# Layer 2's attention: ACT copies the third turn of each cycle ahead of k, q and v, and the third cycle's PSUM banks shift by one place

## The reference, cut to what matters

```
q = (query @ Wq.T + bq).reshape(B, Sq, 16, 16)      # query = layernorm(x)
k = (key @ Wk.T + bk).reshape(B, Skv, 16, 16)       # key = value = ctx_1024
v = (value @ Wv.T + bv).reshape(B, Skv, 16, 16)
q = q * cq + _rotate_half(q) * sq_                  # rotary embedding
k = k * ck + _rotate_half(k) * sk_
scores = jnp.einsum('bqhd,bkhd->bhqk', q, k) * scale
probs = jax.nn.softmax(scores, axis=-1)
ctx = jnp.einsum('bhqk,bkhd->bqhd', probs, v).reshape(B, Sq, H * Dh)
return ctx @ Wo.T + bo
x = x + jnp.tanh(g_xattn[2]) * (the above)
```

## Time and profile before

| what | value |
|---|---|
| median of three runs | 2769.6 us |
| the profiled execution | 2766.18 us, its span 2764.4 us |
| PE busy | 2617.9 us, 95% of the span |
| PEld busy | 1981.6 us, 72% |
| DVE busy | 1547.1 us, 56% |
| ACT busy | 1296.0 us, 47% |
| POOL busy | 642.0 us, 23% |
| layer 2's attention | from about 1320 to 1664 us of the span |

### The profile page before, as it was taken

One profiled execution on the slowest core, in us unless ns is written; L12 is line 12 of the kernel. 1 busy time (PEld: TensorE's weight loads), 2 busy tenths in 40 slices (PEclk: granted clock), 3 DMA queues, 4 the chain that ended last, 5 costly groups with the idle time before them and its releaser, 6 DMA issues. The chain is left out here.

```text
span 2764.4 us, 56714 instructions
## 1 busy us (share of the span) xinstructions
PE 2617.9 (95%) x19818; PEld 1981.6 (72%) x19818; DVE 1547.1 (56%) x4177; ACT 1296.0 (47%) x3610; POOL 642.0 (23%) x626
## 2 busy tenths in 40 slices
PE   6999978999999999989899998999998999989998
PEld 4777756666666666656677766999995777768887
DVE  4777856555555555535787874333235887742222
ACT  4777743343434334331567663333335777732222
POOL 0666661000000000000444431222221111013232
PEclk9999989999999999999999999999999999999999
DMA  3000002000000000010000006999991000059897
GB/s 119 17 23 18 12 2 109 13 13 8 13 7 13 7 13 7 1 34 1 20 18 19 23 7 244 324 334 327 323 326 46 24 18 24 7 201 312 303 312 224
DMA packets 91811, 267.57 MB, mean 97 GB/s; under 512 B 25068, under 2 KB 50804, under 8 KB 77268
## 3 DMA queue, kind: packets, MB, share of 16 engines
q1 hardware_dynamic: 74356, 242.53, 25.4%
q0 software_dynamic: 13632, 18.62, 3.2%
q10 hardware_dynamic: 3616, 3.67, 0.4%
HBM read 248.13 MB, written 16.65 MB: 96 GB/s over the span
## 5 line engine op out<-in xcount | busy, mean ns | idle before, releaser
L825 PEld LDWEIGHTS a_full_ps<-ident,a_probs 112*125 112x125 f32 x2688 | 369.9, 190 | 122.6 <-issue 59.8
L1926 PEld LDWEIGHTS m_banks<-m_x_inT,m_w 128*128 128x128 f32 x3824 | 435.1, 192 | 15.2 <-issue 13.5
L1926 PE MATMUL m_banks<-m_x_inT,m_w 128*128 128x128 f32 x3824 | 442.2, 276 | 1.4 <-ACT m_x_inT L1997 0.9
L936 ACT ACTIVATE a_probs<-a_masked,a_negmax 112x375 f32<-112x375 f32 x512 | 305.4, 598 | 287.7 <-DVE a_negmax L1151 287.7
L825 PE MATMUL a_full_ps<-ident,a_probs 112*125 112x112 f32 x2688 | 417.5, 281 | 16.7 <-ACT a_pT L943 5.6
L1177 DVE COPY a_pT<-a_full_ps 125x448 f32<-125x448 f32 x448 | 277.4, 621 | 233.9 <-PE a_full_ps L825 231.9
L725 PE MATMUL a_full_ps<-attention_room 128*125 128x256 f32 (+1 forms) x960 | 330.0, 472 | 9.6 <-ACT a_qT L926 3.7
L717 PE MATMUL a_full_ps<-attention_room 128*128 128x375 f32 x896 | 325.0, 491 | 13.8 <-PEq L1769 8.6
L1151 DVE CUSTOM_DVE_ANT_0 a_masked<-a_sc_ps,a_mask_add 112x375 f32<-112x375 f32 x512 | 249.7, 544 | 33.2 <-PE a_sc_ps L812 32.0
L936 ACT ACTIVATE a_probs<-a_sc_ps,a_negmax 112x375 f32<-112x375 f32 x384 | 216.6, 575 | 89.4 <-DVE a_negmax L1157 89.3
L843 PEld LDWEIGHTS a_o_ps<-a_pT,a_v 125*32 125x32 f32 (+1 forms) x5376 | 165.2, 118 | 127.0 <-issue 98.7
(11 more groups left out here) (253 smaller groups left out, 3473.3 us busy)
## 6 DMA issues: line engine op xcount, KB each, us to landing
m_w<-in_L2f_w SPq DMA_DIRECT2D x105, 1024.0 KB, 6.4
m_w<-in_L3f_w SPq DMA_DIRECT2D x72, 768.0 KB, 5.9
attention_room<-in_ctxT SPq DMA_DIRECT2D x64, 375.0 KB, 3.1
m_w<-in_L3f_w SPq DMA_DIRECT2D x36, 640.0 KB
m_b<-in_L2f_b SPq DMA_DIRECT2D x35, 128.0 KB, 8.0
p_rows<-normed SPq DMA_DIRECT2D x16, 224.0 KB, 6.2
attention_room<-in_L0x_spline_wT SPq DMA_DIRECT2D x1, 2048.0 KB, 10.5
net_room<-in_L1f_w SPq DMA_DIRECT2D x2, 1024.0 KB
```

The source lines that it names most:

```text
L825: mm = pe.transpose(full_ps[0:KT, bank_of["turn", i, k], (j % 4) * S:(j % 4 + 1) * S], probs[:, i % 2, a, t * KT:(t + 1) * KT], ident[0:S, ...
L936: act.activation(probs[:, i % 2, a, 0:SK], src, ACT.Exp, bias=negmax[:, m:m + 1], scale=-1.0 if mask else 1.0, accum_out=rowsum[:, par, n: ...
L1926: mm = pe.matmul(ab_ps[:, (par * FC + f) % RING, i * SLOTS:(i + 1) * SLOTS], w[:, par, c, f * P:(f + 1) * P], x_inT[:, c, :], start=(c == ...
```

## The change

ACT's body for layer 2 copied, in the first two cycles, k or q first and the third turn last; in the third cycle k 1 stood between the two pairs of exponentials. Now, in all four cycles, the third turn is copied directly behind the last exponential; in the first three cycles k, q and v follow it, and k 1 no longer stands between the exponentials. In the fourth cycle v 1 stays between the pairs, and v 2 follows the turn. In the table of the ring, the rest of the third cycle moves from the head of that cycle to the end of its second turn's place.

```
--- before
+++ after
@@ CYCLES, layer 2
     2: [[[], [("k", 0)], [], [("rest",), ("xT",)]],
         [[], [("q", 0)], [("out",), ("rest",)], []],
-        [[("rest",)], [("k", 1)], [("v", 0, 0)], []],
+        [[], [("k", 1)], [("v", 0, 0), ("rest",)], []],
         [[], [("v", 1, 0)], [("v", 2, 0)], [("rt",)]]],
@@ act body
                         for group in groups:
                             exps(*group, (0, 1))
                         if exists(t) and not copies_last:
                             copy_turn(t, i)
-                        if divided and (not copies_last or i >= 2):
+                        if divided and (not copies_last or i == NG - 1):
                             copies(t, par, i, 1)
                         for group in groups:
                             exps(*group, (2, 3))
                         if copies_last:
-                            if i < 2:
+                            if exists(t):
+                                copy_turn(t, i)
+                            if i < NG - 1:
                                 copies(t, par, i, 1)
                             copies(t, par, i, 2)
-                            if exists(t):
-                                copy_turn(t, i)
```

## The result

The changed kernel takes 2799.03 us, the median of four runs (2798.84 to 2799.22), against 2769.8 of before. The ratio is 1.0105, 95% interval 1.0093 to 1.0118: slower by 29.2 us, where the prediction said 34.6 (2804 us, in the range 2786 to 2814). The profiled execution took 2799.1 us around a span of 2797.3.

What follows compares the result with a forecast made beforehand. PE was taken as the bound. 0.68 + 0.61 + 1.15 = 2.44 us a batch, 34.6 us in all, gave 2800.8 for the profiled execution and 2804 us for the median, range 2786 to 2814 (own range 2794 to 2814).

Steps and rivals of the forecast that it cites:

- The bound and the reserve: Layer 2 attention: PE is the bound, 19.95 of 20.47 us busy; DVE's only reserve is 0.6 us per wait for scores.
- Second cycle, k 0: Late k 0 copy delays its shuffle, the division and P·V: 0.68 us more a batch, bounds 0.55 and 0.75.
- Third cycle, q: Late q copy delays shuffle, row maxima, v 0 and third turn: 6.08 against 5.47 us, 0.61 more, bounds 0.29 and 1.1.
- Fourth cycle, k 1: Late k 1 copy delays shuffle, row maxima and v 2: 6.13 against 4.98 us, 1.15 more, bounds 0.9 and 1.25.
- First cycle: The first cycle itself costs nothing, since k 0's delay shows behind it.
- The ring: Third cycle's moved banks: third turn waits for DVE's second-turn copy, not k 1's; worth nothing either way, bound 0 to 0.05 us.
- The sum: Whole stage: 2.44 us a batch, in full for 14 batches, less for the first two, none for the last: 34.6 us.
- Only the fourth cycle pays: Rival: ACT's copies clear sooner, so only the fourth cycle's 1.15 x 15 = 17 us stay, 2787 us; chance 0.08.
- Not slower: Rival: DVE's idle time absorbs the shuffle delays, the third cycle's exponential wait goes, 2764 to 2766 us; chance 0.06.
- All cancels: Rival: the waits fall where PE has other work and all cancel, about 2770 us; chance 0.04.
- rival four: PE's clock falls in the stage with more idle time, some 40 us and more on top, 2844 us; chance 0.04.

Runs made afterwards that it cites:

- all_shuffles_later: The changed kernel with DVE's shuffles of k and q moved behind row maxima, q's halves behind its second turn: 2769.1 us, 0.9998 of the kernel before.
- divide_first: The changed kernel with DVE's division of the output put ahead of the shuffle of k 0 in the first cycle: 2786.2 us, 1.0062 of the kernel before.
- ring_place_only: The kernel before with only the empty place of the ring moved, ACT's order kept: 2768.9 us, ratio 1.0009.
- turn_last_exps_together: The kernel before with the ring's place moved and, in the third cycle, four exponentials together, then k 1, v 0, third turn last: 2763.0 us, ratio 0.9975.
- k0_behind_turn: The kernel before with ACT copying the third turn ahead of k 0 in the first cycle only, old ring: 2776.3 us, ratio 1.0035.
- k1_v0_behind_turn: The kernel before with, in the third cycle, four exponentials together, then third turn, k 1 and v 0, and the ring's place moved: 2779.2 us, ratio 1.0050.

## Why the prediction was right, step by step

**The bound and the reserve.** PE bounds the stage and DVE had 0.6 us a cycle to spare: right, all_shuffles_later bears it out. But the third cycle was not the only one with a hole in PE. The first has one of 0.28 us ahead of L732 (busy 4.71 of 4.99 us in the earlier trace rows), which I overlooked; it is there after the change too and played no part. ACT's wait of 0.2 us for the first cycle's third turn, which I expected, does not appear; its longer waits in the second and third do (1.18 and 0.88 us).

**Second cycle, k 0.** Predicted 0.68 more through shuffle, division and P·V; measured 5.72 - 5.03 = 0.69, alone as well as in the full change. PE's wait for a_oT is 0.69 us, 13 times. divide_first shows that the division is the whole path.

**Third cycle, q.** Predicted 6.08, measured 5.96. The step is right in all its stations and too long in one: I let the row maxima start 2.05 us after the scores and they start at 1.89. The shuffle begins 0.05 us sooner than I had it (1.31, not 1.36), and the maxima do not wait for the end of the last norm step: they begin at 1413.45, and it ends at 1413.53. v 0 starts at 4.25 instead of 4.43 and the third turn at 5.37 instead of 5.5. That the third turn waits for DVE's copy of the second was in the prediction, and so it is. This is the largest term of the miss: 0.12 us a batch, 1.7 us.

**Fourth cycle, k 1.** Predicted 6.13, measured 6.11; the row maxima at 2.07 instead of the 2.14 I had, v 2 at 4.43 instead of 4.52 after the scores, for the same reason. That the sum is off by 0.02 only is in part luck: from v 2 to the next scores it took 1.68 us where I had 1.61 from the earlier trace rows, and the two errors nearly cancel.

**First cycle.** Nothing predicted, 4.99 as before.

**The ring.** "Worth nothing either way", with a bound of 0 to 0.05 us, is right only for ACT's old order (ring_place_only). Where the third turn's wait for DVE's copy ends last, it costs more: 0.10 us in turn_last_exps_together (5.33 instead of 5.23), so that the 0.24 us that the wait for the exponentials was worth is 0.15 in truth, and 0.14 us in the change as made. The prediction's third cycle had this wait in its chain; only the remark on the ring put it at nothing.

**The sum.** 2.44 us a batch were predicted, 22.78 - 20.47 = 2.31 measured; in the stage 34.6 were predicted, and 32.6 us came up to the last scores. The deductions for the first two batches hold as well: the first costs 1.0 us (predicted 1.1), the second 0.6 less than the later ones (predicted 0.7). The medians differ by only 29.2 us. The two profiled executions differ by 32.9 us; that of before, at 2766.2 us, was itself 3.6 us quicker than the median of 2769.8, while that of the changed kernel lay on its median. I added a difference read in one trace to the median of other executions. It came close enough, but executions of one kernel scatter by as much as this miss, and where the 3.4 us between 32.6 and 29.2 are no trace shows.

**The rivals.** Only the fourth cycle pays: out, each of the three costs by itself. Not slower: out; the gain it lives from exists (0.15 us a batch), and turn_last_exps_together collects it. All cancels: out. The clock: 1.00 throughout the batch, at 90% PE busy (20.58 of 22.78 us), so rival four is out. Its price leaned on a factor of 1.54 to 1.8; no row gives the 1.54, and where the clock stood at 0.50 the same four matmuls took 2.02 instead of 1.09 us, 1.85 times as long. The Trainium skill, "TensorE: Matmul & The Clock Gate", "A second HAM failure mode: psum-queue depth-cycling", has a kernel whose clock swings as PE pauses shortly between groups of matmuls on changing banks. This does not show inside the batches here; PE's pauses of 0.3 to 0.9 us at three banks left the clock at its high level.

## What to carry to other kernels

An engine that copies for others should take first what is ready first, and what the longest queue stands behind. That its own waiting grows says little, as the 34 us of ACT show: with them the stage was as short as before, once no one stood behind them. Before reordering engine A, list for each copy who waits for it on engine B and what is queued behind that waiter: here three shuffles of 0.4 to 0.6 us held the row maxima and a division. And if a copy must be late, move its waiter down in B's queue; exchanging two instructions was worth 10.6 us. And compare stages up to a point ahead of the drain, or its scatter of up to 2.6 us is taken for an effect.

## What the runs showed of the hardware

**A weight load that had to wait for its bank did not run ahead.** In the kernel before, the third turn's first weight load began 0.21 us before its first matmul:

```profile
1410.94 0.62 PEld L825 LDWEIGHTS a_full_ps<-ident,a_probs 112*125 112x125 f32 x4
```

The matmul came at 1411.15, 0.05 us after the end of DVE's copy of the second turn (1411.10), for which it did not have to wait. When the turn waits for a copy, load and matmul begin within 0.03 us of each other (1474.27 and 1474.30), the first 0.12 us after the copy's end. The four transposes take 0.66 instead of 0.59 us, and the next scores come 0.10 us later than by the sum of the steps. A wait that was expected to end just in time was so not free.

**The end of the stage runs at either level of the clock.** The last output projection of the stage, the same four matmuls, in the kernel before and in the changed one:

```profile
1662.09:1663.20 1.11, 1.09 (x4) 0.59 (x4) 0.00 (x0) 0.00 (x0) 0.00 (x0) 1.00 0.00 0
```

```profile
1694.42:1696.44 2.02, 2.02 (x4) 1.04 (x4) 0.00 (x0) 0.00 (x0) 0.00 (x0) 0.50 0.00 0
```

Five of the twelve traces have 2.02 us there (after, k0_behind_turn, ring_place_only and the two with the later shuffles of k), the others 1.09, and it does not follow what was changed. The whole drain ahead of it took 9.37 to 9.88 us in the five traces whose clock stayed at 1.00 there, and 10.64 to 11.97 us in the other seven, at a mean clock of 0.84 down to 0.70. Here it is in k1_v0_behind_turn and in ring_place_only, whose PE has the same two pauses in the drain up to where they part (1.28 and 0.63 us):

```profile
1664.88:1674.76 9.88, 6.70 (x108) 4.98 (x107) 5.55 (x13) 4.31 (x12) 0.94 (x2) 1.00 0.01 2
```

```profile
1653.13:1665.10 11.97, 9.33 (x108) 7.09 (x107) 5.71 (x13) 4.29 (x12) 0.95 (x2) 0.71 0.01 1
```

What decides between the two levels the runs do not show. Each such draining can so move the time by a microsecond or two, and this may be part of the scatter of 2763 to 2771 us that the kernel before showed over its runs; that was not tested.
